# An AdaLN block with a softmax-gated scan and experts: the softmax row sums are split between GpSimd and VectorE, and three kinds of VectorE instructions get longer

## The reference

```
h   = layernorm(x) * (1 + ca) + sa
x   = x + ga * attn(h)
h   = layernorm(x) * (1 + cb) + sb
x   = x + gb * ffn(h)

attn(h):  hn = rmsnorm(h) * norm_w;  v = hn @ W_v.T          # 8 heads of 16
          gates = softmax((hn @ W_a.T) as [head, 16, 17])    # rows of 17
          a0 = gates[..., 0];  A = gates[..., 1:]            # A is 16x16 per head
          state_t = A_t @ state_(t-1) + a0_t * v_t           # in order of t
          return h + states @ W_out.T
ffn(h):   top 4 of 8 experts, softmax weights
          gate, up = split(h @ gate_up[e]);  gate = min(gate, 7);  up = clip(up, -7, 7)
          act = (up + 1) * gate * sigmoid(1.702 * gate)
          out = sum over experts of weight * (act @ down[e].T + bias)
```

## Time and profile before

| | us |
|---|---|
| median of 3 runs | 925.56 (924.06 to 926.71) |
| profiled execution, whole | 925.54 |
| its span | 923.8 |
| VectorE busy | 785.9 (85%), 2313 instructions |
| GpSimd busy | 590.8 (64%), 667 instructions |
| TensorE busy | 637.9 (69%) |
| ScalarE busy | 529.3 (57%) |

### The profile page before, as it was taken

How to read it: one execution, slowest core, us unless ns; L and a number is a source line. 1 busy time by engine, 2 the same in 40 slices (tenths; PEclk the granted TensorE clock), 3 DMA queues, 4 the chain that set the end, 5 groups by cost and what they waited for, 6 DMA issues and landing times.

```text
span 923.8 us, 11922 instructions
## 1 busy us (share of the span) xinstructions
PE 637.9 (69%) x2762; PEld 473.4 (51%) x2762; DVE 785.9 (85%) x2313; ACT 529.3 (57%) x1203; POOL 590.8 (64%) x667
## 2 busy tenths in 40 slices
PE   5662332586976868585967767685968867587886
PEld 4320111364755646373745646473756646466776
DVE  3464999999999999989899999999999999898641
ACT  3443221476674747566674747575765747474786
POOL 0484737386767678586767678586757666653454
PEclk9876666698887879798897979697887879698998
DMA  7027637463644455553644445554634454553100
GB/s 214 14 54 160 149 74 162 90 136 74 135 82 102 91 109 115 112 123 71 145 77 104 95 98 115 120 115 77 149 77 112 89 99 90 115 126 55 23 12 7
DMA packets 101670, 91.60 MB, mean 99 GB/s; under 512 B 43688, under 2 KB 98272, under 8 KB 99424
## 3 DMA queue, kind: packets, MB, share of 16 engines
q1 hardware_dynamic: 101600, 90.84, 46.2%
HBM read 46.76 MB, written 41.94 MB: 96 GB/s over the span
## 4 chain that ended last, share of the span: by engine, by line
DVE 53%; PE 28%; POOL 8%; issue 6%; SPq 2%; DMA 2%; ACT 1%; DVEq 0%; POOLq 0%; ACTq 0%
DVE prod L778 13%; DVE ps L786 12%; PE ps L1010 12%; DVE zs L761 8%; PE ps L1023 8%; DVE act_t L859 5%; DVE nmax L754 4%; PE ps L997 4%; DVE xh L748 3%; POOL lg L414 2%; PE ps L1056 2%; DVE rz L769 2%; POOL rs L393 1%; DMA gu_rows<-_L_ffn_gate_up_proj_dram 1%; SPq L330 1%
## 5 line engine op out<-in xcount | busy, mean ns | idle before, releaser
L1010 PE MATMUL ps<-h2t,wgu 128*128 128x256 f32 x1024 | 281.5, 424 | 4.3 <-ACT up L618 4.3
L1023 PE MATMUL ps<-wd,act_t 128*128 128x128 f32 x1024 | 161.2, 307 | 137.8 <-DVE act_t L859 137.8
L1010 PEld LDWEIGHTS ps<-h2t,wgu 128*128 128x128 f32 x1024 | 217.3, 218 | 66.8 <-issue 29.6
L1023 PEld LDWEIGHTS ps<-wd,act_t 128*128 128x128 f32 x1024 | 145.7, 214 | 172.0 <-DVE act_t L859 158.7
L778 DVE TENSOR_TENSOR prod<-gates,ps 64x272 f32<-64x272 f32 x512 | 214.4, 419 | 17.5 <-DMA gates<-gate_dram 14.4
L786 DVE TENSOR_REDUCE ps<-prod 64x16 f32<-64x272 f32 x512 | 220.2, 430 | 9.9
L997 PE MATMUL ps<-wl,ht 128*128 128x512 f32 (+1 forms) x320 | 174.7, 651 | 57.9 <-ACT lg L601 48.5
L460 POOL TENSOR_TENSOR yacc<-yacc,weighted 128x256 f32<-128x256 f32 x128 | 93.0, 726 | 93.3 <-ACT weighted L635 92.2
L414 POOL TENSOR_TENSOR lg<-lg,nmax 128x1088 f32<-128x1088 f32 x64 | 130.3, 2039 | 7.4 <-DVE nmax L754 3.5
L407 POOL TENSOR_TENSOR ex<-ex,rz 128x1088 f32<-128x1088 f32 x64 | 129.7, 2039 | 6.4 <-DVE rz L769 4.1
L859 DVE SCALAR_TENSOR_TENSOR act_t<-ps,up 128x256 f32<-128x256 f32 x256 | 97.9, 410 | 41.6 <-ACT ps L624 34.4
(11 more groups left out here) (119 smaller groups left out, 587.6 us busy)
## 6 DMA issues: line engine op xcount, KB each, us to landing
gate_dram<-ex SPq DMA_DIRECT2D x256, 136.0 KB, 3.0
gates<-gate_dram SPq DMA_DIRECT2D x32, 1088.0 KB, 8.3
yt_tok<-y_dram SPq DMA_DIRECT2D x256, 8.0 KB, 5.5
xg<-in_L_attn_x_dram SPq DMA_DIRECT2D x32, 64.0 KB
out_dram<-res SPq DMA_DIRECT2D x32, 64.0 KB
y_dram<-ys SPq DMA_DIRECT2D x32, 64.0 KB, 2.0
r_in<-out_dram SPq DMA_DIRECT2D x32, 64.0 KB
xm<-xn SPq DMA_DIRECT2D x16, 128.0 KB, 3.1
```

The costliest lines, as they stand in the source:

```text
L1010: last = nc.tensor.matmul(gu_ps(m, k, which)[:, q * N:(q + 1) * N], wgu[:, k, rows + q * P:rows + (q + 1) * P], h2t[:, m % 2, :], start=Tr ...
L1023: last = nc.tensor.matmul(dn_ps(j), act_t[:, k % 2, q * N + j * P:q * N + (j + 1) * P], wd[:, k, q, :], start=(q == 0), stop=(q == KI - 1))
```

## The change

- New GpSimd work `fold_row`: for each tile, when the exponentials are there, a tile `fold` of [128 rows x 8] is filled with elements 1 to 8 plus elements 9 to 16 of each row (one instruction of 1,024 elements), and then element 0 of the row is added to the first of the eight (one of 128 elements, which waits for the first). Both tiles are folded in a row, ahead of gate_value of tile 0 and clamp_up of expert 0.
- VectorE's `row_sum` sums rows of 8 of `fold` instead of rows of 17 of `ex`, in 2 instructions of 64 rows per tile instead of 8 of 16, at positions 17, 18 and 23, 24; it waits for fold_row of its tile. `row_inverse` of tile 0 goes from position 18 to 20. gate_value no longer waits for the sums.
- `row_max` takes 32 rows (544 elements) in an instruction instead of 16 (272), 4 per tile instead of 8, at positions 36, 39, 43, 48 and 54, 59, 63, 66.
- `hidden` takes both halves of an expert in one instruction of 512 columns, at the position of the first half (25, 34, ...). Its wait for dn_done goes.

```diff
+            def fold_row(e, j):
+                pool.wait_ge(exp_ok.sem, exp_ok.at(e, j + 1))
+                if not is_first(e):
+                    pool.wait_ge(zs_ok.sem, zs_ok.at(e - 1, 2 * j + 2))
+                v = ex[:, j, :].rearrange("p (r k) -> p r k", k=M1)
+                nc.gpsimd.tensor_tensor(fold[:, j, :, :], v[:, :, 1:1 + M // 2], v[:, :, 1 + M // 2:M1], ALU.add
+                                        ).then_inc(half_ok.sem, 1)
+                pool.wait_ge(half_ok.sem, half_ok.at(e, j + 1))
+                nc.gpsimd.tensor_tensor(fold[:, j, :, 0], fold[:, j, :, 0], v[:, :, 0], ALU.add).then_inc(fold_ok.sem, 1)
+
             def gate_value(e, j):
-                pool.wait_ge(zs_ok.sem, zs_ok.at(e, H * (j + 1)))
...
                 if o is not None:
                     finish(o)
                 if e is not None:
+                    fold_row(e, 0)
+                    fold_row(e, 1)
                     gate_value(e, 0)
                 if m is not None:
                     clamp_up(m, 0)
...
-            def row_sum(e, j, h):
-                if h == 0:
-                    dve.wait_ge(exp_ok.sem, exp_ok.at(e, j + 1))
-                nc.vector.tensor_reduce(zs[:, j, h * M:(h + 1) * M],
-                                        ex[:, j, h * M * M1:(h + 1) * M * M1].rearrange("p (r k) -> p r k", k=M1),
-                                        AX_X, ALU.add).then_inc(zs_ok.sem, 1)
+            def row_sum(e, j, half):
+                dve.wait_ge(fold_ok.sem, fold_ok.at(e, j + 1))
+                rows = slice(half * HI // 2, (half + 1) * HI // 2)
+                nc.vector.tensor_reduce(zs[:, j, rows], fold[:, j, rows, :], AX_X, ALU.add).then_inc(zs_ok.sem, 1)
...
-            def hidden(m, k, q):
-
-                if q == 0:
-                    dve.wait_ge(sg_ok.sem, sg_ok.at(m, k + 1))
-                    dve.wait_ge(clamp_ok.sem, clamp_ok.at(m, k + 1))
-                    if k >= 2:
-                        dve.wait_ge(dn_done.sem, dn_done.at(m, k - 1))
-                    elif not is_first(m):
-                        dve.wait_ge(dn_done.sem, dn_done.at(m - 1, E + k - 1))
-                cols = slice(q * N, (q + 1) * N)
-                nc.vector.scalar_tensor_tensor(out=act_t[:, k % 2, cols], in0=gu_ps(m, k, 1)[:, cols], scalar=SILU_LIMIT,
-                                               in1=up[:, k % 2, cols], op0=ALU.min, op1=ALU.mult).then_inc(act_ok.sem, 1)
+            def hidden(m, k):
+                dve.wait_ge(sg_ok.sem, sg_ok.at(m, k + 1))
+                dve.wait_ge(clamp_ok.sem, clamp_ok.at(m, k + 1))
+                nc.vector.scalar_tensor_tensor(out=act_t[:, k % 2, :], in0=gu_ps(m, k, 1), scalar=SILU_LIMIT,
+                                               in1=up[:, k % 2, :], op0=ALU.min, op1=ALU.mult).then_inc(act_ok.sem, 1)
...
                 if e is not None:
-                    if 9 <= u < 17:
-                        row_sum(e, 0, u - 9)
-                    if u == 18:
+                    if u in (17, 18):
+                        row_sum(e, 0, u - 17)
+                    if u == 20:
                         row_inverse(e, 0)
...
```

More of the change, by code:

```diff
@@ L67, in adaln_block @@
     KL = -(-NL // LC)
+    NQ = 4
+    QR = HI // NQ
     STEP_INCS = 2
@@ L134, in adaln_block @@
         ex = sb("ex", [P, TILES, NG])
+        fold = sb("fold", [P, TILES, HI, M // 2])
         zs = sb("zs", [P, TILES, HI])
@@ L411, in sub_max @@
                 lo, hi = part * HI // 2, (part + 1) * HI // 2
-                pool.wait_ge(nmax_ok.sem, nmax_ok.at(g, H * j + H // 2 * (part + 1)))
+                pool.wait_ge(nmax_ok.sem, nmax_ok.at(g, NQ * j + NQ // 2 * (part + 1)))
                 v = lg[:, j, :].rearrange("p (r k) -> p r k", k=M1)[:, lo:hi, :]
@@ L888, in between @@
                 if g is not None:
-                    if 33 <= u < 49 and u % 2:
-                        row_max(g, 0, (u - 33) // 2)
-                    if 53 <= u < 69 and u % 2:
-                        row_max(g, 1, (u - 53) // 2)
+                    if u in (36, 39, 43, 48):
+                        row_max(g, 0, (36, 39, 43, 48).index(u))
+                    if u in (54, 59, 63, 66):
+                        row_max(g, 1, (54, 59, 63, 66).index(u))
                 if a is not None:
```

35 lines of the change are left out of this document (17 added, 18 removed).

## The result

The change makes the kernel slower: **948.8 us** (median of 4 runs, 947.28 to 949.66) against 924.81 for the kernel before on the same chip (922.81 to 926.71), a ratio of 1.0264 [1.0245, 1.0283], +24.0 us. The forecast was 939.5 with a range of 928 to 952: the direction and the path of the loss are right, the size is some ten microseconds short.

The account below looks back on a forecast made before the run. A passage hangs on when expert 0's first act_t is finished, 1.5 us later behind the folds. Passages 6 to 15 +14.0, passage 2 +3.3, less small gains: +13.9 on the 925.56 median, 939.5 us; range 928 to 952.

Parts of the forecast that it names:

- What bounds a passage: One pipeline pass: VectorE bounds xh to first expert product (now 1.5 us later), TensorE thence to go, VectorE mostly the rest.
- Position of the folds: GpSimd folds follow finish(o), ahead of gate_value and clamp_up of expert 0; VectorE waits 4.0 us before its first sum.
- The price of the fold: On GpSimd per tile: 1,024-element add 1.94 us, 0.08 late start, dependent 128-element add 0.52; 2.54 us in all.
- Rival (b): GpSimd's wide add, with two full streams, costs 2.9 us: +1.0 a passage, about 951 us; chance 0.16.
- Passages 3, 4, and the tail: Passages 3 and 4 gain 0.4 us, passages 16 and 17 gain 1.0, the tail's merged products 1.0.
- The fixed part of a VectorE instruction: 0.08 us per instruction in a full queue; 0.35 us spacing at 272 elements leaves no room for 156 ns.
- VectorE's busy time: Sign of being right: VectorE's busy total falls by more than 80 us while the kernel's time rises.
- TensorE's wait ahead of the down matmuls: Sign of being right: TensorE's idle time before the first down matmuls grows by about 1.5 us.
- The gains behind the wait: Third stretch, after go: GpSimd's subtraction still stops xh of stage p; no gain before that, then two products save 0.06 each.
- (a): Rival: folds stay out of the way before the first expert product and VectorE's shorter queue shows; 891 us, chance 0.08.
- (c): Rival: loss partly given back, by a 1.2 us wide add or VectorE beating GpSimd's subtraction; 931 to 932 us, chance 0.11.
- (d): Rival: VectorE's queue shortens as the change says and the two effects cancel; 925.5 us, chance 0.05.

Follow-up runs that it names:

- e4: The change with finish(o) moved behind clamp_up of expert 0 on GpSimd, so the folds start earlier: 925.01 us, ratio 1.0003.
- e0_forms: The changed kernel with fourteen GpSimd adds of different operand forms behind the last output, to time each; ran once, 971.15 us with the adds in it.
- e2: The kernel before with only the longer maxima and expert products; sums of 17 stay on VectorE, no fold: 918.2 us, ratio 0.9925.
- h2: The kernel before with only expert 0's two product halves moved from positions 25 and 26 to 19 and 20 on VectorE: 884.69 us, ratio 0.9567.
- g1: The kernel of e2 with only expert 0's product moved from position 25 to 19 on VectorE: 875.16 us, ratio 0.9458.
- h1: g1 with one tile's sums from a GpSimd fold behind finish(o), itself moved behind clamp_up of expert 0; second reciprocal at position 25: 882.67 us, ratio 0.954.

## Why the forecast was right in direction and short in size

**What bounds a passage: right.** The first stretch decided: the product ends 2.10 us later. The second is TensorE's (12.72 before and after, from product to go). The third shrank by 0.2 us in the mean and by 0.13 between its shorter lengths (26.70 to 26.57); the forecast had 0.12.

**Position of the folds: right.** They follow finish(o) with no gap, VectorE waits 4.41 us before its first sum (4.0 forecast), the second pair of sums doesn't wait, and from the first sum to the start of the product it is 5.46 us (5.45 forecast). e4 shows it from the other side: with finish(o) out of the way 23.8 of 24.0 us are back.

**The price of the fold: the term that was mis-sized.** I put the wide add at 1.94 us by the 1,088-element multiply and the narrow one at 0.52 by gate_value's row. They measured 2.45 and 0.66, together 0.65 us more a fold (a wide add above 2.4 was one of the forecast's own signs of being wrong). The first fold alone delays VectorE: 0.6 on the product's end (13.95, forecast 13.34 when counted from the start of xh), so 2.0 a passage and not 1.4, 20 us over ten; passages 6 to 15 measured 19.5. In passage 2 both folds stand in the way: +3.3 + 2 x 0.65 = 4.6 of the 5.6; the last 1.0 is not traced. With the measured prices the forecast's sum would have come to 939.5 + 6 + 1.3, near 947. The multiply was nearest in length, but one of its operands repeats; e0_forms shows what that is worth. Rival (b), which had this reason and put the add at 2.9, gave 951, and the measured 948.8 lies nearer to it than to the forecast. That is in part luck: its 2.9 was about as far above the 2.45 as my 1.94 was below, and what it put on too much makes up for the 2 us that the forecast lacked elsewhere. The Trainium skill's two-input figure (GPSIMD Engine Reference, Elementwise), which makes 2.3 us of 1,024 elements, an estimate by that page, was set aside in the forecast; the gapless add measured 2.34, and the slope and fixed part of e0_forms give 4.49 us at 2,048 elements against the page's 4,497 ns, so the trace agrees with it, and my slope from the rows, which joined a full-stream add to a repeating multiply, was the wrong one.

**Passages 3, 4, and the tail: 2 us short in all.** Forecast -2.4 for these, measured -0.6. Passage 3 came out at +0.4, passage 16 at +1.0. I let the folds count for nothing there; no run takes these passages apart.

**The fixed part of a VectorE instruction: half right.** The forecast said that the trace leaves no room for the Trainium skill's dispatch of about 156 ns (GPSIMD Engine Reference, Elementwise). That holds for the spacing in a full queue. The duration does have it: 418 - 272 x 0.97 = 154 ns; neighbours in the queue overlap by about half of it. e2, with 256 instructions fewer, gained 6.9 us, far from a full 156 ns for each (40 us).

**VectorE's busy time: wrong.** "More than 80 us" less was the sign, 56.8 came. The 86 us by which the three groups' busy times fall (102.3 to 42.9, 104.7 to 88.8, 97.9 to 87.0) are sums of durations that overlap their neighbours, and the page counts the overlap once; the same working, with 0.35 us a slot, had been used correctly for the queue. A forecast of engine totals has to use the spacing too.

**TensorE's wait ahead of the down matmuls: wrong.** The sign was 1.5 us more idle time there; it fell, from 5.07 to 4.44 in the mean. In between TensorE turns the router's weights (comb), which VectorE now computes behind the wait for the fold, so the growth is in the wait before that (before, then after):

```profile
537.12 0.59 PE L1051 MATMUL ps<-ident,comb 128*8 128x128 f32 x2 [2.50 <-DVE comb L845]
...
554.51 0.59 PE L1055 MATMUL ps<-ident,comb 128*8 128x128 f32 x2 [5.16 <-DVE comb L858]
```

With the wait for act_t (5.00, now 4.44) the two make 7.50 and 9.60: 2.1 more, as the product's end is. The other signs follow from the price: the product ends after 13.95 (13.2 to 13.5), the period is 53.49 (53.0).

**The gains behind the wait: right, none.** xh of stage p ends with GpSimd's subtraction in both kernels. Rivals (a), (c) and (d) did not occur.

**A way that the forecast did not look for.** VectorE's queue ahead of the first product is what a passage hangs on, and the forecast took the work ahead of it as given. The sums of the second tile are not needed by the product (those of the first are, in the kernel before: gate_value waits for them, and clamp_up of expert 0 stands behind it). Moving the product past six of the second tile's sums (h2) is worth 40 us, six times what the longer instructions alone are (e2).

## What to carry to other kernels

Before work is handed to an idle engine, ask where in that engine's queue it will stand and who waits behind it: 96 us of GpSimd's free time were used here to make the kernel slower, and moving three small instructions of the same queue took nearly all of the loss away. The time to compare with is that of the rest of the change alone: by it (e2) the folds cost 31 us where they stood and still 7 in the better place. Where a product that another engine waits for stands behind work that it does not need, move that one instruction, but only to where its own inputs are ready; moved past that, it holds up the whole queue. Price an operation by a row with the same kind of operands, and only then by the nearest length.

## What the runs showed of the hardware that was not expected

- A GpSimd add in float32 with two full input streams, without gaps, takes 2.10 ns an element and 0.19 us, from 128 to 1,088 elements (e0_forms). With one operand that repeats each value 8 times, 1,024 elements take 1.96 us and not 2.34.
- The order of a strided add matters more than its gaps: the fold's own elements with the index of 8 outermost took 4.00 us, against 2.45:

```profile
952.02 4.00 POOL L592 TENSOR_TENSOR fold<-ex 128x1024 f32<-128x1024 f32 x1
```

- VectorE's tensor_scalar xh (128 x 128, float32) takes 0.33 us, but 0.60 to 1.99 where a GpSimd instruction is under way as it starts and goes on for longer. There are 132 such cases in the fourteen traces, 120 beside the 2.04 us subtraction and 12 beside an accumulate, and in each xh ends 0.08 us after the GpSimd instruction. So semaphores are not the only ties between the queues. VectorE's sums, maxima and scan products beside the same long instructions show no such stop (a median of 0.42 us each for 272 elements, with them and without). In g1 against h1, by this sum, it decides which is faster: a VectorE that comes 0.9 us sooner ends 0.7 later, and 0.4 more is lost behind it.
